# Softmax maxima moved into free PSUM columns, and ScalarE's order in the odd slots, in a perceiver block

## The reference

```python
q = (x @ Wq).reshape(B, Nq, HEADS, DIM_HEAD)          # x is layer-normed
k = (context @ Wk).reshape(B, context.shape[1], HEADS, DIM_HEAD)
v = (context @ Wv).reshape(B, context.shape[1], HEADS, DIM_HEAD)
sim = jnp.einsum('bihd,bjhd->bhij', q, k) * SCALE
attn = jax.nn.softmax(sim, axis=-1)
out = jnp.einsum('bhij,bjhd->bihd', attn, v)
```

## Time and profile before

| what | value |
|---|---|
| median of 3 runs | 966.65 us (965.09 to 969.07) |
| the profiled execution's own time | 967.87 us |
| its span in the profile | 965.8 us |
| PE busy | 912.1 us, 94% of the span |
| DVE busy | 642.5 us, 67% |
| ACT busy | 596.9 us, 62% |
| POOL busy | 508.6 us, 53% |

### The profile page before, as it was taken

How to read it: one execution, slowest core, us unless ns; L and a number is a source line. 1 busy time by engine, 2 the same in 40 slices (tenths; PEclk the granted TensorE clock), 3 DMA queues, 4 the chain that set the end, 5 groups by cost and what they waited for, 6 DMA issues and landing times.

```text
span 965.8 us, 17868 instructions
## 1 busy us (share of the span) xinstructions
PE 912.1 (94%) x6354; PEld 459.8 (48%) x6354; DVE 642.5 (67%) x1085; ACT 596.9 (62%) x1126; POOL 508.6 (53%) x394
## 2 busy tenths in 40 slices
PE   7999999999989999999999999999898899999998
PEld 4444445444544544454445444444443455554444
DVE  6546665666666566656665666678777778886634
ACT  4757767767677766777677668666675712326540
POOL 2535566556645755565467556767796586310000
PEclk9999999999999999999999999999899999999999
DMA  9346766756656566655656766987888546134501
GB/s 327 77 88 120 124 131 153 151 120 127 137 121 126 134 139 128 126 137 134 133 142 134 134 130 137 185 198 143 174 148 170 110 68 140 26 108 88 168 19 76
DMA packets 340263, 126.24 MB, mean 131 GB/s; under 512 B 316113, under 2 KB 317905, under 8 KB 340177
## 3 DMA queue, kind: packets, MB, share of 16 engines
q1 hardware_dynamic: 324032, 94.30, 48.8%
q10 hardware_dynamic: 16144, 30.81, 10.4%
HBM read 45.36 MB, written 2.10 MB: 49 GB/s over the span
## 4 chain that ended last, share of the span: by engine, by line
PE 71%; DVE 13%; ACT 7%; issue 3%; POOL 1%; SPq 1%; DMA 1%; ACTq 0%; DVEq 0%; POOLq 0%
PE v_ps L679 21%; PE k_ps L679 20%; PE e_ps L748 7%; PE e_ps L679 7%; DVE run L1535 5%; PE o_ps L769 4%; DVE q_max L1532 4%; PE e_ps L1034 3%; PE o_ps L772 2%; ACT p_h L1199 2%; ACT v L1164 2%; PE o_ps L1027 2%; DVE v L1517 2%; PE e_ps L1027 1%; ACT p_f L1201 1%
## 5 line engine op out<-in xcount | busy, mean ns | idle before, releaser
L1981 POOL TENSOR_TENSOR p_l<-p_f,p_h 128x1024 f16<-128x1024 f32 x128 | 274.4, 2144 | 268.9 <-ACT p_f L1201 266.0
L1199 ACT ACTIVATE p_h<-e_ps,bias 128x512 f16<-128x512 f32 x256 | 176.7, 690 | 6.2 <-issue 4.0
L1201 ACT ACTIVATE p_f<-e_ps,bias 128x512 f32<-128x512 f32 x256 | 177.3, 693 | 0.0
L1521 DVE TENSOR_TENSOR k_l<-k_ps,k_h 128x512 f16<-128x512 f32 x128 | 88.4, 691 | 128.3 <-ACT k_h L1170 128.3
L1517 DVE TENSOR_TENSOR v<-v_ps,v 128x512 f16<-128x512 f32 x127 | 87.9, 692 | 100.7 <-ACT v L1164 100.5
L679 PE MATMUL v_ps<-wv_h,ctx_h 128*128 128x512 f16 (+1 forms) x384 | 103.0, 377 | 30.5 <-DVE v L1517 30.5
L1532 DVE TENSOR_REDUCE q_max<-e_ps 128x2 f32<-128x1024 f32 x96 | 117.2, 1221 | 7.8 <-PE e_ps L748 2.1
L1176 ACT ACTIVATE bias<-run 128x2 f32<-128x2 f32 x128 | 26.0, 203 | 150.6 <-DVE run L1535 127.7
L679 PE MATMUL k_ps<-ctx_h,wk_h 128*128 128x512 f16 x384 | 105.0, 383 | 9.0 <-DVE k_l L1521 8.7
L769 PE MATMUL o_ps<-v,pt_h 128*128 128x129 f16 x1024 | 106.8, 221 | 2.0 <-DMA pt_l<-p_l 2.0
L679 PE MATMUL k_ps<-ctx_h,wk_l 128*128 128x512 f16 x384 | 105.1, 383 | 0.0
(11 more groups left out here) (311 smaller groups left out, 1363.2 us busy)
## 6 DMA issues: line engine op xcount, KB each, us to landing
raw<-in_ctx_t ACTq DMA_DIRECT2D x29, 768.0 KB, 5.1
w_raw<-in_w_t SPq DMA_DIRECT2D x32, 256.0 KB, 3.7
pt_h<-p_h SPq DMA_TRANSPOSE x128, 3.2
pt_l<-p_l SPq DMA_TRANSPOSE x128, 3.1
out<-xr SPq DMA_DIRECT2D x7, 256.0 KB, 2.0
x_in<-in_x SPq DMA_DIRECT2D x6, 256.0 KB, 9.4
raw<-in_ctx_t SPq DMA_DIRECT2D x2, 768.0 KB, 9.7
o_all<-in_x ACTq DMA_DIRECT2D x6, 256.0 KB, 4.5
```

What stands on the lines that cost most here:

```text
L1199: act.activation(p_h[:, s % H_RING, h, :], e_ps[s % 2][:, h, :], ACT.Exp, scale=EXP_SCALE, bias=bias[:, i % 2, p, h:h + 1]).then_inc(p_hi, 1)
L1201: act.activation(p_f[:, s % F_RING, h, :], e_ps[s % 2][:, h, :], ACT.Exp, scale=EXP_SCALE, bias=bias[:, i % 2, p, h:h + 1]).then_inc(p_ful ...
L1521: dve.tensor_tensor(k_l[:, s % K_RING, :], k_ps[:, :], k_h[:, s % K_RING, :], ALU.subtract).then_inc(k_split, 1)
L1981: pool.tensor_tensor(p_l[:, s % L_RING, :, :], p_f[:, s % F_RING, :, :], p_h[:, s % H_RING, :, :], ALU.subtract).then_inc(p_split, 1)
```

## The change

`q_max` moves from SBUF to four free columns of the PSUM bank `o_ps[1]` (columns 384 to 387; the weighted values use columns 0 to 258), two for an even slot and two for an odd one. `run` is then made from a PSUM and an SBUF operand. `gap` was the difference of two SBUF tensors and one instruction; now DVE first writes the minimum of `q_max` and the old `run` into four more PSUM columns (`least`) and then subtracts the old `run` from that: two instructions, each with a PSUM and an SBUF operand. `gap_ready` so counts two for each pair. Before it starts the weighted values of an odd slot (which begin with a product that starts a new sum in bank `o_ps[1]`), PE now waits until the gap of the pair has been made. On ACT, in odd slots from 3 on (slot 3 itself takes a path of its own that is left as it was), `v_high(s+1)` moves ahead of the bias of x and of the first exponentials.

```diff
+        q_max, least = o_ps[1][:, 384:388], o_ps[1][:, 388:392]
...
             def weighted_values(s):
...
+                if s + 1 in GAPS:
+                    pe.wait_ge(gap_ready, 2 * gaps_at(s + 1) + 2)
...
             def steady(s):                       # ACT
...
+                if pair and s + 1 < SLOTS and s > 1:
+                    v_high(s + 1)
                 if ahead:
                     if pair:
                         quarter_bias(x)
                     exps(x, 0)
                     if pair:
                         quarter_bias(x + 1)
-                if 0 < s and s + 1 < SLOTS:
+                if 0 < s and s + 1 < SLOTS and (s == 1 or not pair):
                     v_high(s + 1)
...
             def quarter_maximum(s):
...
-                dve.tensor_reduce(q_max[:, s % 2, :], e_ps[s % 2][:, :, :], AX, ALU.max, negate=True).then_inc(q_maxed, 1)
-                dve.wait_ge(q_maxed, PAIRS * (i - 1 - i // QUARTERS) + p + 1)
+                own = q_max[:, 2 * (s % 2):2 * (s % 2) + 2]
+                dve.tensor_reduce(own, e_ps[s % 2][:, :, :], AX, ALU.max, negate=True).then_inc(q_maxed, 1)
+                dve.wait_ge(q_maxed, 2 * gaps_at(s - s % 2) + s % 2 + 1)
                 dve.wait_ge(e_maxed, s - PAIRS + 1)
-                dve.tensor_tensor(run[:, i % 2, p, :], q_max[:, s % 2, :], run[:, 1 - i % 2, p, :], ALU.min).then_inc(e_maxed, 1)
+                dve.tensor_tensor(run[:, i % 2, p, :], own, run[:, 1 - i % 2, p, :], ALU.min).then_inc(e_maxed, 1)
...
             def gaps(s):
...
-                dve.wait_ge(e_maxed, s + 2)
+                before = run[:, 1 - i % 2, p:p + 2, :].rearrange("p a h -> p (a h)")
+                dve.wait_ge(q_maxed, 2 * gaps_at(s) + 2)
+                dve.tensor_tensor(least, q_max, before, ALU.min).then_inc(gap_ready, 1)
+                dve.wait_ge(gap_ready, 2 * gaps_at(s) + 1)
                 if gaps_at(s) >= 4:
                     dve.wait_ge(fade_ready, gaps_at(s) - 3)
-                dve.tensor_tensor(gap[:, i % 2, p:p + 2, :], run[:, i % 2, p:p + 2, :], run[:, 1 - i % 2, p:p + 2, :],
-                                  ALU.subtract).then_inc(gap_ready, 1)
+                dve.tensor_tensor(gap[:, i % 2, p:p + 2, :].rearrange("p a h -> p (a h)"), least, before, ALU.subtract)\
+                    .then_inc(gap_ready, 1)
```

More of the change, by code:

```diff
@@ L68, in perceiver_kernel @@
         ("stats", [P, B, 6], F32), ("mean_var", [P, B, 2], F32), ("rstd", [P, B], F32), ("exponent", [P, B], F32),
-        ("q_max", [P, 2, 2], F32), ("run", [P, 2, PAIRS, 2], F32), ("bias", [P, 2, PAIRS, 2], F32), ("gap", [P, 2, PAIRS, 2], F32),
+        ("run", [P, 2, PAIRS, 2], F32), ("bias", [P, 2, PAIRS, 2], F32), ("gap", [P, 2, PAIRS, 2], F32),
         ("fade", [P, 2, PAIRS, 2], F32), ("acc", [P, PAIRS, 2, VW], F32), ("o_rec", [P, PAIRS, 2, 1], F32), ("o_sum", [P, 2, DH], F32),
@@ L164, in perceiver_kernel @@
     (o_all, ident, causal, bo_row, bv_row, b2_row, bq_col, bk_col, b1_col, b2_half, stats, mean_var, rstd, exponent,
-     q_max, run, bias, gap, fade, acc, o_rec, o_sum, o_f,
+     run, bias, gap, fade, acc, o_rec, o_sum, o_f,
      ones, bq_half, bk_half, bias_prod, u_col, w_col, w_half, s_col, c_sum, c_col,
@@ L1181, in fades_of @@
                 i, p = unit_of(s)
-                act.wait_ge(gap_ready, gaps_at(s) + 1)
+                act.wait_ge(gap_ready, 2 * gaps_at(s) + 2)
                 if i >= 2:
```

## The result

The changed kernel takes **938.25 us** (median of 3 runs, 937.67 to 938.33) against 966.65 us before (965.09 to 969.07): the ratio is 0.9702, 95% interval 0.9669 to 0.9734, so it is 3.0% faster. The prediction was 933.5 us, in a range of 924 to 950. The profiled execution took 938.25 us too; its span is 936.4 us.

A forecast was written before the change was run, and what follows sets the result against it. PE, busy 94%, was held up by DVE instructions with two SBUF inputs waiting for POOL. Terms -28.0 + 11.4 - 15.4 - 1.2 = -33.2 us took 967.87 to 934.7, less 1.2 to 933.5 us; range 924 to 950.

The forecast's parts named there:

- step (5): Pairs 51 to 61: run and gap no longer wait for POOL, weight_low still can; -15.4 us, bounds -10 and -18.4.
- correction for the profiled execution: Whole kernel: the median of the runs is 1.2 us lower than the profiled execution, so 934.7 becomes 933.5 us.
- Step (3): ACT's order in odd slots: PE waits 0.19 us in each of 60 pairs, +11.4 us, bounds 0 to +30.
- Step (6): Behind the last pair: PE's wait for fold_low, behind a gap that waits for POOL, goes; -1.2 us.
- Step (1): Maxima in PSUM: run falls from 2.44 to about 0.16 us in 18 long pairs, -28.0 us.
- Rival D: The PSUM operand does not keep DVE off POOL, none of the 44.6 us is won: 978 us, chance 0.05.
- Step (2): Two DVE instructions for the gap: 7.7 us more DVE time in 48 slots, covered by idle time, cost 0.
- Rivals A and B: ACT's new order: A, it costs nothing, 922, chance 0.12; B, some 0.4 us a pair, 946, chance 0.15.
- Step (4): PE's wait for the gap before an odd slot's weighted values is always over when reached: 0.
- The waits that I left: Pairs 51 to 61: one wait of weight_low in pair 55 and one in 59, 3 us of the 18.4 lost there.
- Granted clock 1.00 throughout: Sign in the profile after: with waits this short in pairs 51 to 61 PE should keep its clock, 0.96 before.
- Rival C: The last pairs keep most waits, POOL's backlog meeting weight_low alone: 12 us less gain, 945 us, chance 0.12.

The follow-up runs named there:

- PSUM-only kernel: Maxima and gaps in PSUM as in the changed kernel, ACT's order in odd slots as before the change: 927.25 us, ratio 0.9594.
- control in one kernel: Against the kernel with only the PSUM part, gap alone goes back to one instruction on two SBUF tensors, run stays: 928.81 us, ratio 0.9611.
- order-only kernel: The kernel before the change with ACT's new order alone, maxima and gaps in SBUF: 960.25 us, ratio 0.9941.
- kernel with one bias moved back: The changed kernel with the first bias, and it alone, ahead of v_high in odd slots: 927.05 us, ratio 0.9591.
- run with copies: The changed kernel with sixteen transposes of attention weights on SyncE's list made plain copies, result not the reference's: 933.37 us, ratio 0.9666.
- PSUM-only kernel with the output's transposes moved: Maxima and gaps in PSUM, ACT's old order, the seventh output's two transposes behind slot 121 instead of 116: 923.91 us, ratio 0.9571.

## Why the prediction was right, and where it was off

Its direction, its mechanism and its two large terms hold; it was 4.8 us too low. 3.7 us of that lie in one term, step (5), and 1.2 in the correction for the profiled execution; what is off in steps (3) and (6) nearly cancels.

- **Step (1), maxima in PSUM, -28.0.** Right: 49 pairs in the PSUM-only kernel take 522.83 us, 27.96 less than in the earlier trace rows. The control in one kernel (0.161 us against 3.06), and the 36 instances beside `ctx_low` that still take 0.16 us, show that the two SBUF inputs are the cause. The Trainium skill ("GPSIMD Engine Reference", Specifications) names the SBUF interfaces that GpSimd shares with VectorE and the contention with DVE instructions that have two SBUF inputs, and these traces agree: 2.44 us where `run` had two, 0.16 where it has one. Rival D is out.
- **Step (2), two instructions for the gap, 0.** Right for the time. They take 0.16 us each. The 12 us of DVE time that the prediction estimated from the Trainium skill's fixed extra for PSUM ("VectorE: DVE Perf Modes", TRN2 errata) are not seen: a median `run` takes 159 ns with a PSUM input and took 161 with two in SBUF, a gap 161 against 152. The reduction's median is 1225 ns with its result in SBUF (the order-only kernel) and 1233 in PSUM.
- **Step (3), ACT's order, +11.4.** Right: 4.79 us from keys to keys where 4.77 was foretold, 0.21 us in a pair where 0.19 was. That the whole comes so near (11.0 us between the PSUM-only kernel and the changed one) is in part luck: the 49 pairs cost 10.2 where 9.3 was foretold, the last eleven 0.6 where it was 2.1. The kernel with one bias moved back shows that it is this chain. That the waits would be listed as PE's for `k_low` was wrong: the period shows them, PE's idle times don't. Rivals A and B are out.
- **Step (4), PE's wait for the gap, 0.** Right: no row of PE's waits names `gap`.
- **Step (5), pairs 51 to 61, -15.4.** This is the mis-sized term. With the +2.1 that (3) adds to eleven pairs it should have been -13.3; it is -9.6. The PSUM-only kernel, which has no part of (3), shows the term by itself: 135.78 - 125.55, so -10.2 for -15.4. The waits that I left were 3 us of the 18.4; the changed kernel has 6.5. Two waits for `k_low` came, in pairs 55 and 58, and make these pairs 2.6 us longer, but only the first is of the kind that I named, a `weight_low` that waits for `ctx_low`; the second is POOL's leading half that comes late. What I did not see are transposes of probabilities that stand in SyncE's list behind weights and output, 2.11 us of waiting in pair 59, and the granted clock of 0.86 behind it, which makes pair 60 1.6 us longer. "Granted clock 1.00 throughout" was wrong with it. I had gone through SyncE's queue for step (3) only, in a stretch where it has sixteen transposes of weights and two of the output less. The last eleven pairs got 0.9 us shorter each, and the issues in them did not; the run with copies shows that making the sixteen issues shorter (0.68 us for 1.34) gives 4.3 of the 6.5 us back. Rival C was right that more waits stay, and POOL, which it named, is behind the one in pair 58; its 945 was far too high.
- **Step (6), the end, -1.2.** It is -2.0: the wait of 1.21 us for `fold_low` has gone, as the earlier trace rows let expect. Most of the rest is PE's wait for the last low half of the probabilities, 1.18 us where it was 1.96; no term had it.
- *The sum.* -28.0 + 11.4 - 15.4 - 1.2 = -33.2 was foretold against the profiled 967.87 us; it is 938.25 - 967.87 = -29.6, and 3.6 us of the gap between 933.5 and 938.25 are in these terms. The other 1.2 were taken off because that execution lay above its median; the changed kernel's lay at its own.

The prediction had no term for what the two parts are worth one without the other, and the order-only run shows why it should: the same move on ACT that costs 11.0 us behind the PSUM part saves 6 us without it.

## What to carry to other kernels

When a change takes away the reason for which another part of it was made, measure the parts apart: here one half brings 39 us, the other gives 11 of them back. In this kernel a chain over two engines that was 0.03 us shorter than PE's own work (by the sum of its steps) was free, and one that was 0.2 us longer cost that in every pair. Such a chain can be added up from the starts in a timeline before it is built. Where a stretch gets shorter, go through every queue of that stretch once more, the DMA issues above all, since they do not shrink with it.

## What the runs showed of the hardware

- A DVE instruction of 128x4 elements with two SBUF inputs took up to 3.06 us beside POOL's work, and four of its five long instances ended 0.02 us behind POOL's instruction; one of 128x2 with one input in PSUM took 0.161 us at most, in the same kernel. In the changed kernel that one took 0.16 us also in the 36 of 96 cases in which POOL was at work on `ctx_low` when it started.
- A small DVE instruction costs nearly the same from PSUM as from SBUF (128x2: 159 and 161 ns; 128x4: 161 and 152), and a reduction of 128x1024 that writes two elements a row takes 8 ns more into PSUM (1233 against 1225).
- An issue of a transpose takes SyncE 1.19 to 1.34 us in most cases, but one in ten took over 1.7 in the changed and in the PSUM-only kernel, and single ones up to 3.83 (the PSUM-only kernel with the output's transposes moved); they occur ahead of pair 51 as well. One of a plain copy of the same halves took 0.68 (sixteen in 10.9 us).
- Behind an idle time of PE's of 2.11 us the granted clock of the next pair was 0.86; behind one of 1.97 us, in the kernel with the first bias ahead, it was 1.00 (third number from the end):

```profile
692.80:703.47 10.67, 10.67 (x82) 5.39 (x81) 7.28 (x15) 7.17 (x15) 7.17 (x5) 1.00 1.12 179
```
